# Bias centring, head scales, last feed-forward ticks and norm statistics moved inside a decoder layer kernel

## The reference

```python
v = (xv @ Wv.T + bv)                       # heads of N = 8 channels
mu = z.mean(-1, keepdims=True)             # z: attention output y by head
var = z.var(-1, keepdims=True)
zn = ((z - mu) * jax.lax.rsqrt(var + EPS)).reshape(Bx, Tx, Cx)
y = (zn * ln_g + ln_b) * g
return y @ Wo.T + bo
...
x = x + attn(_layernorm(x), ...)
x = x + xattn(_layernorm(x), ctx, ...)     # softmax(q k) v @ Wout.T
x = x + ffn(_layernorm(x), ...)            # silu(x Wg) * (x Wu), scaled by the router, @ Wd
```

## Time and profile before

| what | value |
|---|---|
| median of 3 runs | 692.47 us |
| the profiled execution's own time | 690.42 us |
| its span | 688.7 us |
| TensorE busy (matmuls) | 631.9 us, 92% |
| DVE, POOL, ACT busy | 56%, 49%, 39% |
| mean clock granted to TensorE | 0.973 of full speed |

### The profile page before, as it was taken

One profiled execution on the slowest core, in us unless ns is written; L12 is line 12 of the kernel. 1 busy time (PEld: TensorE's weight loads), 2 busy tenths in 40 slices (PEclk: granted clock), 3 DMA queues, 4 the chain that ended last, 5 costly groups with the idle time before them and its releaser, 6 DMA issues.

```text
span 688.7 us, 16278 instructions
## 1 busy us (share of the span) xinstructions
PE 631.9 (92%) x6728; PEld 507.3 (74%) x6728; DVE 384.4 (56%) x780; ACT 269.7 (39%) x608; POOL 339.0 (49%) x474
## 2 busy tenths in 40 slices
PE   7887876799999999799999999799999999889997
PEld 6444455446979899545888889655879789779996
DVE  5997778688524554678533554779634244442120
ACT  4956123233234545242335545142334445143332
POOL 7673154223555656314455565313455555407666
PEclk9999989899999999999999999999999999979999
DMA  8911000020121111020120121011111111004220
GB/s 197 358 35 31 1 2 1 1 63 10 40 77 37 40 55 29 15 61 10 41 77 25 43 57 35 17 25 40 38 41 36 40 47 40 13 23 129 63 73 16
DMA packets 41540, 34.15 MB, mean 50 GB/s; under 512 B 9613, under 2 KB 40918, under 8 KB 41466
## 3 DMA queue, kind: packets, MB, share of 16 engines
q1 hardware_dynamic: 39562, 31.27, 16.3%
q10 hardware_dynamic: 1904, 1.84, 0.8%
HBM read 30.92 MB, written 2.17 MB: 48 GB/s over the span
## 4 chain that ended last, share of the span: by engine, by line
PE 53%; DVE 19%; POOL 14%; issue 7%; ACT 5%; DMA 1%; ACTq 0%; POOLq 0%; DVEq 0%
PE bank L984 6%; DVE A L1426 6%; PE bank L988 5%; PE bank L989 4%; PE bank L990 4%; PE bank L1156 4%; PE bank L1228 3%; POOL A L679 3%; POOL hT_last L687 3%; PE bank L1023 3%; DVE nm L1495 3%; POOL hb L599 3%; PE bank L1090 2%; PE bank L1025 2%; PE bank L1024 2%
## 5 line engine op out<-in xcount | busy, mean ns | idle before, releaser
L1401 DVE TENSOR_TENSOR hb<-hb,bank 128x256 f32<-128x256 f32 x102 | 42.5, 417 | 145.6 <-ACT hb L761 145.6
L589 POOL TENSOR_TENSOR hT<-hb,hT 128x256 fp32r<-128x256 f32 x102 | 78.2, 766 | 72.9 <-ACT hT L751 72.9
L599 POOL TENSOR_TENSOR hb<-hb,cwb 128x256 f32<-128x256 f32 x102 | 75.1, 736 | 78.1 <-DVE hb L1401 78.1
L751 ACT ACTIVATE hT<-hb 128x256 fp32r<-128x256 f32 x102 | 42.4, 416 | 131.3 <-POOL hb L599 131.3
L988 PE MATMUL bank<-xTf,wGh 128*128 128x256 f32 x272 | 83.5, 307 | 0.0
L1426 DVE TENSOR_TENSOR A<-bank,decay 128x512 f32<-128x512 f32 x128 | 77.4, 681 | 8.2 <-PE bank L1079 8.2
L989 PE MATMUL bank<-xTf,wGh 128*128 128x256 f32 x272 | 77.1, 284 | 0.0
L990 PE MATMUL bank<-xTf,wGl 128*128 128x256 f32 x272 | 77.0, 283 | 0.0
L989 PE MATMUL bank<-xTf,wUh 128*128 128x256 f32 x272 | 77.0, 283 | 0.0
L988 PE MATMUL bank<-xTf,wUh 128*128 128x256 f32 x272 | 76.9, 283 | 0.0
L990 PE MATMUL bank<-xTf,wUl 128*128 128x256 f32 x272 | 76.7, 282 | 0.0
(11 more groups left out here) (215 smaller groups left out, 1428.9 us busy)
## 6 DMA issues: line engine op xcount, KB each, us to landing
cwb<-cw_rows SPq DMA_DIRECT2D x54, 128.0 KB, 2.9
A<-cw_rows SPq DMA_DIRECT2D x18, 128.0 KB, 3.2
A<-in_x SPq DMA_DIRECT2D x4, 512.0 KB, 4.8
res<-in_x SPq DMA_DIRECT2D x4, 512.0 KB, 4.4
out_x<-res SPq DMA_DIRECT2D x8, 256.0 KB, 2.4
rawG<-in_L_ffn_w_gate SPq DMA_DIRECT2D x2, 704.0 KB, 7.0
rawU<-in_L_ffn_w_up SPq DMA_DIRECT2D x2, 704.0 KB, 7.2
cwb<-cw_rows SPq DMA_DIRECT2D x12, 112.0 KB, 2.8
```

What stands on the lines that cost most here:

```text
L589: pool.tensor_tensor(hT[:, c % 2, 1, :], hb[:, c % 2, :], hT[:, c % 2, 0, :].bitcast(F32), ALU.subtract).then_inc(h_lo, 1)
L599: pool.tensor_tensor(hb[:, c % 2, :], hb[:, c % 2, :], cwb[:, c % CWS, :], ALU.mult).then_inc(h_scaled, 1)
L751: act.activation(hT[:, c % 2, 0, :], hb[:, c % 2, :], ACT.Copy).then_inc(h_hi, 1)
L1401: tt(hb[:, c % 2, :], hb[:, c % 2, :], PS[5 + c % 2][:, HT:GT], ALU.mult).then_inc(gu_used, 1)
```

## The change

It has four parts.

1. v's bias: its DMA is issued third on SP, ahead of nine small ones; its sum by head and the scaling of that stand on DVE between the first norm's statistics and its application, the subtraction behind the application. Before, all three stood between the mixed inputs 5 and 6.
2. The head scales of group 0 go to banks 4 to 7 in place of 0 to 3, so that the `headsel` products no longer wait for the key tiles and the four value copies (L1465), and the copies move behind L1476 on DVE. The second half of the output projection, which writes bank 0, waits for the copies. The low part 0 moves from the place n2 to x0a.
3. Ticks: every group has the same counts. In groups 1 and 2 one tick less lies at n2 and one at n5, so that ticks 5 to 9 lie one tick later and those behind them two. Behind the cross attention's output projection come ticks 31 and 32 (r0), then `gate_up(33)`, the third norm's turn, `down(31)`, `down(32)` (r2), the first projection of the next group, and `down(33)` (r3). In group 3 the same, with r3 behind the router's products. On DVE tick 32 stands ahead of `layer_apply`.
4. Second and third norm: after each half of the residual (two sequences) its own statistics and aggregates.

```diff
--- before.py
+++ after.py
@@ -372,19 +372,17 @@
...
-        POINTS = ["n0", "n1", "n2", "n3", "n4", "n5"] + [f"x{b}{p}" for b in range(GB) for p in "abc"] + ["y0", "r0", "r1"]
-        COUNT = dict(n0=1, n1=2, n2=3, n3=2, n4=2, n5=2, y0=1, r0=3, r1=1)
+        POINTS = ["n0", "n1", "n2", "n3", "n4", "n5"] + [f"x{b}{p}" for b in range(GB) for p in "abc"] + ["y0", "r0", "r1", "r2", "r3"]
+        COUNT = dict(n0=1, n1=2, n2=2, n3=2, n4=2, n5=1, y0=1, r0=2, r1=1, r2=1, r3=2)
...
                 COUNT[f"x{b}{p}"] = k
-        LAST = dict(COUNT, n2=2, n5=1, r0=5)
-        assert sum(COUNT.values()) == sum(LAST.values()) == TICKS
+        assert sum(COUNT.values()) == TICKS
...
-            count = LAST if g == NG - 1 else COUNT
-            first = sum(count[p] for p in POINTS[:POINTS.index(point)])
-            return range(first, first + count[point])
+            first = sum(COUNT[p] for p in POINTS[:POINTS.index(point)])
+            return range(first, first + COUNT[point])
@@ -393,7 +391,7 @@
...
         HIGH_AT = dict(n1=(3, 4), n2=(5, 6, 7))
-        LOW_AT = dict(n2=(0,), n5=(1, 2, 3), x0a=(4, 5), x2a=(6, 7))
+        LOW_AT = dict(n5=(1, 2, 3), x0a=(0, 4, 5), x2a=(6, 7))
@@ -402,11 +400,11 @@
...
             sp.dma_start(td, time_decay.partition_broadcast(P)).then_inc(decay_in, 16)
+            sp.dma_start(bvB[:], bv.partition_broadcast(P)).then_inc(bias_in, 16)
...
             sp.dma_start(tf, time_faaaa.partition_broadcast(P)).then_inc(row_in, 16)
-            sp.dma_start(bvB[:], bv.partition_broadcast(P)).then_inc(bias_in, 16)
@@ -465,8 +463,8 @@
...
                 point(g, "y0")
-                point(g, "r0")
-                point(g, "r1")
+                for name in ("r0", "r1", "r2", "r3"):
+                    point(g, name)
...
@@ -892,6 +890,8 @@
...
                     act.activation(xTf[:, 0, k, :], PS[k][:, :], ACT.Copy).then_inc(xTf_hi, 1)
+                point(g, "r2")
+                point(g, "r3")
@@ -1133,24 +1133,29 @@
...
                     idle_product(10, 7)
-                pe.wait_ge(kbd_ready, g * 4 + 4)
-                pe.wait_ge(xvp_ready, g * 4 + 4)
+                if g:
+                    pe.wait_ge(kbd_ready, g * 4 + 4)
+                    pe.wait_ge(xvp_ready, g * 4 + 4)
                 pe.wait_ge(gn_step, g * GN_STEPS + GN_STEPS)
+                spread = 0 if g else 4
...
                         rows = slice(32 * b, 32 * b + 32)
-                        last = mm(PS[b][:, m * P:(m + 1) * P], headsel[rows, m, :], gn_y[rows, :], start=True, stop=True,
+                        last = mm(PS[spread + b][:, m * P:(m + 1) * P], headsel[rows, m, :], gn_y[rows, :], start=True, stop=True,
...
                 if g == 0:
-                    idle_product(6, 7)
+                    pe.wait_ge(kbd_ready, 4)
+                    idle_product(6, 1)
...
                                 pe.wait_ge(*ready[k])
+                            elif g == 0 and src is gact and k == 0:
+                                pe.wait_ge(xvp_ready, 4)
@@ -1258,10 +1263,17 @@
...
                 point(g, "r0")
+                if g:
+                    n = ticks_at(g, "r1")[0]
+                    assert n == FN - 1
+                    gate_up(g - 1, n)
                 turn_norm(2, g, tok2, 0)
-                point(g, "r1")
+                if g:
+                    down(g - 1, n - 2)
+                point(g, "r2")
...
                     project(g + 1, 0)
+                    point(g, "r3")
@@ -1272,6 +1284,8 @@
...
                     project(g + 1, 1)
+                else:
+                    point(g, "r3")
@@ -1303,6 +1317,17 @@
...
+            def half_stats(s, src, q):
+                i = 0 if s == 0 else 1
+                for b in (2 * q, 2 * q + 1):
+                    nc.vector.bn_stats(st[:, i, b, :], src[:, b, :]).then_inc(ln_stats[s], 1)
...
+            def half_means(s, g, q):
+                i = 0 if s == 0 else 1
+                dve.wait_ge(ln_stats[s], g * 4 + 2 * q + 2)
+                for b in (2 * q, 2 * q + 1):
+                    nc.vector.bn_aggr(mv[:, i, b, :], st[:, i, b, :]).then_inc(ln_mean[s], 1)
@@ -1328,8 +1353,15 @@
...
             layer_stats(0, 0, tokx)
+            dve.wait_ge(bias_in, 16)
+            bv_head = bvB[:].rearrange("p (h n) -> p h n", n=N)
+            nc.vector.tensor_reduce(b_mean, bv_head, AX, ALU.add).then_inc(head_step, 1)
+            dve.wait_ge(head_step, 2)
+            ts(b_mean, b_mean, 1.0 / N, None, ALU.mult).then_inc(head_step, 1)
...
             layer_apply(0, 0, tokx, tokx)
+            dve.wait_ge(head_step, 3)
+            tt(bv_head, bv_head, b_mean.unsqueeze(2).to_broadcast([P, H, N]), ALU.subtract).then_inc(head_step, 1)
...
@@ -1456,13 +1481,18 @@
...
                     norm_step(n)
-                dve.wait_ge(xvp_zero, g * 2 + 2)
-                for e in range(2):
-                    dve.wait_ge(vp_ready, g * 2 + e + 1)
-                    for w in range(2):
-                        src = PS[3 if e == 0 else 0][:, :].rearrange("p (b h w d) -> p b h w d", b=2, w=2, d=XD)
-                        dst = xvp[:, e:GB:2].rearrange("p b (h w) n -> p b h w n", w=2)
-                        nc.vector.tensor_copy(dst[:, :, :, w, XD * w:XD * w + XD], src[:, :, :, w, :]).then_inc(xvp_ready, 1)
...
+                def take_values():
+                    dve.wait_ge(xvp_zero, g * 2 + 2)
+                    for e in range(2):
+                        dve.wait_ge(vp_ready, g * 2 + e + 1)
+                        for w in range(2):
+                            src = PS[3 if e == 0 else 0][:, :].rearrange("p (b h w d) -> p b h w d", b=2, w=2, d=XD)
+                            dst = xvp[:, e:GB:2].rearrange("p b (h w) n -> p b h w n", w=2)
+                            nc.vector.tensor_copy(dst[:, :, :, w, XD * w:XD * w + XD], src[:, :, :, w, :]).then_inc(xvp_ready, 1)
...
+                if g:
+                    take_values()
@@ -1470,17 +1500,20 @@
...
                     y3 = ysb[:, m, :].rearrange("p (b t) -> p b t", b=GB)
-                    stt(y3, y3, cols[:, LNG, m:m + 1], PSB[:, 0:GB, m * P:(m + 1) * P], ALU.mult, ALU.mult).then_inc(y_normed, 1)
+                    stt(y3, y3, cols[:, LNG, m:m + 1], PSB[:, 0 if g else 4:GB if g else 8, m * P:(m + 1) * P], ALU.mult, ALU.mult).then_inc(y_normed, 1)
...
+                if g == 0:
+                    take_values()
...
-                dve.wait_ge(x1_ready, g * 2 + 2)
-                layer_stats(1, g, X)
+                    dve.wait_ge(x1_ready, g * 2 + q + 1)
+                    half_stats(1, X, q)
+                    half_means(1, g, q)
@@ -1544,16 +1577,16 @@
...
-                dve.wait_ge(x2_ready, g * 2 + 2)
-                layer_stats(2, g, X)
+                    dve.wait_ge(x2_ready, g * 2 + q + 1)
+                    half_stats(2, X, q)
+                    half_means(2, g, q)
...
                     mixed_input(g + 1, 0)
+                if g:
+                    ffn_tick(g - 1, ticks_at(g, "r0")[1])
                 layer_apply(2, g, X, tok2)
-                if g:
-                    for n in ticks_at(g, "r0")[1:]:
-                        ffn_tick(g - 1, n)
...
```

More of the change, by code:

```diff
@@ L1357, in take_v @@
                         if g == 0:
-                            dve.wait_ge(head_step, 6)
+                            dve.wait_ge(head_step, 4)
                     tt(vt[:, 2 * q:2 * q + 2, :], pair(PS[2 if q == 0 else 3]), bvB[:].unsqueeze(1).to_broadcast([P, 2, C]),
@@ L1368, in _ @@
             nc.vector.tensor_reduce(v_sum, by_head, AX, ALU.add).then_inc(head_step, 1)
-            dve.wait_ge(head_step, 2)
+            dve.wait_ge(head_step, 5)
             ts(v_mean, v_sum, 1.0 / N, None, ALU.mult).then_inc(head_step, 1)
-            dve.wait_ge(head_step, 3)
+            dve.wait_ge(head_step, 6)
             for k in range(KC):
@@ L1377, in _ @@
             mixed_input(0, 5)
-            dve.wait_ge(bias_in, 16)
-            bv_head = bvB[:].rearrange("p (h n) -> p h n", n=N)
-            nc.vector.tensor_reduce(b_mean, bv_head, AX, ALU.add).then_inc(head_step, 1)
-            dve.wait_ge(head_step, 4)
-            ts(b_mean, b_mean, 1.0 / N, None, ALU.mult).then_inc(head_step, 1)
-            dve.wait_ge(head_step, 5)
-            tt(bv_head, bv_head, b_mean.unsqueeze(2).to_broadcast([P, H, N]), ALU.subtract).then_inc(head_step, 1)
             mixed_input(0, 6)
```

1 line of the change is left out of this document (removed).

## The result

| kernel | median | executions | lowest to highest |
|---|---|---|---|
| before | 692.72 us | 4 | 691.09 to 692.98 |
| changed | 671.21 us | 4 | 669.73 to 674.65 |
| changed, once more (below) | 674.22 us | 5 | 671.02 to 674.82 |

The ratio is 0.9701 (95% interval 0.9659 to 0.9744), in a later batch 0.9737 (0.9715 to 0.9759); the nine executions of the changed kernel have their middle at 672.2. So by the medians the change takes 21.5 us off in the first batch and 16.8 in the later one, whose kernel before had 690.97. The profiled execution of after took 672.13 us against 690.42 of before, 18.3 less. I account for those 18.3, since only the profiled execution has a trace.

A forecast was written before the change was run, and what follows sets the result against it. TensorE, busy 92%, was taken as the bound. Groups 1 and 2 -2.4, group 3 -8.0, group 0 -1.4 and -0.9, low part 0 +1.0, bias +0.3 summed to -11.4 us: 681.0 us, range 675 to 688.

The forecast's parts named there:

- step (c): Groups 1 and 2, `down(17)` waiting for the add to res: 3.6 us lost each, 1.7 wait and 1.9 lower clock.
- (a) n2 and n5: Groups 1 and 2, value copies to query projection: two ticks less, 5.1 us gained a group.
- (b) the third norm: Groups 1 and 2, output projection's end to router's products: reordered ticks bring the router's products 0.3 us later.
- rival B: TensorE's clock holds: -3.1 us each in groups 1 and 2, -8.8 in group 3; 676.5 us, chance 0.20.
- Group 3: Last group, output projection's end to the router's second turn: 25.6 us becomes 17.0; -8.0 taken.
- Part 4: Halved statistics: second norm 0, third norm of group 0 -0.9 us; groups 1 to 3 counted elsewhere or hidden by ticks.
- Part 2: Group 0, value copies leave the chain between head norm and `headsel` products: -1.4 us.
- Low part 0: Moved to x0a, where DVE's low parts compete with POOL's causal cuts: +1.0 us, between 0 and 1.6.
- Part 1: The moved bias work on DVE meets POOL's selects in a short gap ahead of the mixed inputs: +0.3 us.
- Rival C: The clock also falls at the third norm's turn: sum -5.3 us, 687 us, chance 0.20.
- E: Slower: third norm's application behind tick 32 at least 3.8 us late in each of three groups; chance 0.05.

The follow-up runs named there:

- changed, once more: The changed kernel with nothing edited, profiled and timed a second time: 674.22 us.
- part 3 alone: The kernel before with only the tick counts and the ticks round the third norm's turn changed: 680.91 us (ratio 0.9856).
- the rest alone: The kernel before with parts 1, 2 and 4 and low part 0 at x0a, but the old ticks: 682.42 us (ratio 0.9884).
- the add ahead: The changed kernel with DVE's add of the FFN's first half to res moved ahead of tick 18's product: 666.59 us (ratio 0.9645).

## Why the prediction was wrong, point by point

Direction, places and waits came out as forecast; the sum was short by 6.9 us of 18.3, and by 5.4 and 10.1 in the medians of the two batches. Two things failed: the clock term of step (c), and the halves of the second norm, which I had put at nothing.

**(a) n2 and n5**: -5.1 forecast. The stretch gave -5.8 in group 1, of which 0.7 is the second norm (below). Right.

**(b) the third norm**: +0.3 forecast, 0.0 measured. Right in its steps: application at 5.6 us behind the projection (5.7), bound by tick 32's product. Its 0.4 and 0.3 us of waiting never drew the clock down.

**(c) `down(17)`: this step failed.** "Loss 3.6 us in each of groups 1 and 2, of which 1.7 is sure and 1.9 is clock." The wait was 1.69 and 1.70 us; the 1.9 did not come at all, since the clock held in both groups. I took one fall behind one wait in the trace of before as what such a wait does. In kernels with both norms in halves, as the changed one, none of 16 waits of that length has a fall. Two groups at 1.9 make 3.8 of the 6.9 us. With it goes 1.6 that I did not count: group 3 of before had the fall and could get it back, and did (75.74 to 74.12). Together 5.4 us. This was rival B, at 0.20. Its 676.5 us had neither group 3's share nor that of the halves, and lies 5.3 above the median of 671.2 and 2.3 above the later 674.2. That part 3 alone has the two falls I forecast does not save the step: it was said of the whole change.

**Group 3**: -8.0 forecast, -8.3 measured, of which part 3 alone gives 7.6. Right. The stretch from the end of the output projection to L1299 takes 17.1 us; I had 17.0.

**Part 4**: "halved statistics of the second norm hide behind these products: 0" was said of group 0, and for groups 1 to 3 "in (b) or hidden by ticks". Wrong for the second norm of groups 1 to 3, where ticks do not hide it: 0.7, 0.3 and 0.7 us, 1.6 in all. Whole again, this one edit cost 5 us by the medians. In group 0 the third norm's application starts 0.8 us sooner behind the start of the output projection (7.38 us for 8.16); I had 0.9.

**Part 2**: -1.4 forecast. The output projection of group 0 starts 1.4 us sooner (65.03 for 66.40) and the query projection 1.5. Right. (The copies' 1.41 us stand in the earlier trace rows, of groups 1 and 3, and not in the earlier trace rows.) **Low part 0**: +1.0 forecast, 1.2 as a wait and 2.5 with the clock. POOL lost 1.2 of the 1.62 us, so on the wait my bound of 0 to 1.6 held, and the clock came on top. The Trainium skill (SBUF — State Buffer, SBUF: two separate sides) has the shared port pair taken for a whole instruction, which I priced at +1.6. The trace agrees in kind: `ve` takes 1.19 us beside DVE's subtractions and 0.22 without them.

**Part 1**: +0.3 forecast, 0 measured: group 0's first scores start at 31.27 us for 31.30. The three bias instructions lie in the gaps of the first norm, and the scaling takes 0.18 us there.

**Rival C** (the clock falls at the turn, too) did not occur in any group of the two profiles: waits of 0.4 and 0.3 us at the turn are far from the 3.7 behind which it fell in groups 1 and 2 of before. The Trainium skill (TensorE: Matmul & The Clock Gate, HAM oscillation — how this bites in real kernels) describes waits that repeat and lower the clock each time. The trace does not show it for the waits at the turn, which repeat in three groups. **E** needed an application at least 3.8 us later than I had it, and it came within 0.1.

The medians moved by 16.8 and 21.5 us in the two batches, the profile by 18.3. Group 0 differs by 2.4 us between the two profiles of the changed kernel, mostly by its clock, and that is the size of the difference.

## What to carry over

Split a lower clock from the wait ahead of it, and count how often the same wait has it, in the kernel that you price: one row is one draw. A wait on the engine that bounds costs its length, and 1.7 us more where the clock falls behind it: here never (0 of 16) at 1.7 us in kernels with both norms in halves, 5 times of 10 in the others, 3 of 3 at 3.7. So shortening several waits a little can pay more than the sum of the lengths: part 3 alone and the rest alone each had two falls in groups 1 to 3 where the kernel before had six, in one profile each. Before you move work into an idle gap, ask what made the gap: the 4.3 us on DVE went away with the slow cuts that had caused it.

## What the hardware showed that I had not expected

Whether the clock falls behind a wait of this size cannot be told from the wait. In the profiles of before and of part 3 alone, group 3's wait ends at the same time (545.54 and 545.55 us, 1.71 and 1.73 us long) behind the same work; the clock fell in the first and held in the second. Each single fall lacks 1.7 us of full clock, whatever the wait was. And a wait can hide a fall: in the first group `attend` of step 1 starts 11.26 us behind the first key scores in the profile of the add ahead, where TensorE ran at its lower clock between them and waits 1.57 us, and 11.27 in that of the changed kernel, where it ran at full clock and waits 3.26. The fall ahead of the wait cost nothing; the one behind it, 1.3.
